# GNN kernel on one core: the table of places for W's products in 16-bit integers

## The reference

```python
edge_index = jnp.stack([src, dst])
h = jnp.maximum(_layernorm(x), 0.0)
# L0: row, col = edge_index
W = jnp.zeros((1024, 1024)).at[row, col].add(edge_weight)
x = x + h @ W.T + L0_gnn_bias
h = jnp.maximum(_layernorm(x), 0.0)
# L1, twice with its own weights (relu between): agg = segment_sum(h[src], dst)
#   h @ W_self + (agg / max(deg, 1)) @ W_neigh + b
x = x + L1_gnn(h, src, dst, ...)
```

## Time and profile before

| | |
|---|---|
| median of 3 runs | 769.54 us (769.11 to 769.72) |
| the profiled execution | 768.53 us |
| its span, first to last instruction | 766.5 us |
| granted TensorE clock in it | 1.0 of full speed, in every slice |
| PE busy | 747.6 us, 98% of the span |
| DVE, POOL, ACT busy | 75%, 62%, 46% |

### The profile page before, as it was taken

The page is one execution under the profiler, slowest core; times in us unless marked ns, Lnnn a source line. Parts: engine busy times, 40 slices in busy tenths (PEclk is TensorE's granted clock), DMA queues, the critical chain, the costliest instruction groups (busy, mean ns, idle before and its releaser), DMA issues.

```text
span 766.5 us, 13521 instructions
## 1 busy us (share of the span) xinstructions
PE 747.6 (98%) x4453; PEld 620.8 (81%) x4454; DVE 572.1 (75%) x819; ACT 353.5 (46%) x593; POOL 473.6 (62%) x593
## 2 busy tenths in 40 slices
PE   3999999999999999999999999999999999999998
PEld 2878888888888888888788888888888888887887
DVE  7999677877465797986779685446598857569885
ACT  7977623433353452366336745542223323245731
POOL 3000366667579999865656373436999875645992
PEclk9999999999999999999999999999999999999999
DMA  3123467665586854567683536776743868785475
GB/s 117 50 74 111 115 217 257 204 227 179 167 289 198 295 157 133 172 218 253 211 271 116 165 120 197 253 247 208 272 142 104 254 199 286 234 288 185 144 235 202
DMA packets 82984, 148.78 MB, mean 194 GB/s; under 512 B 10809, under 2 KB 21108, under 8 KB 82912
## 3 DMA queue, kind: packets, MB, share of 16 engines
q1 hardware_dynamic: 62974, 105.18, 44.0%
q10 hardware_dynamic: 19938, 42.69, 15.8%
HBM read 106.42 MB, written 41.41 MB: 193 GB/s over the span
## 4 chain that ended last, share of the span: by engine, by line
PE 97%; DVE 2%; issue 1%; DMA 0%; DVEq 0%
PE bank L1765 50%; PE bank L1819 21%; PE bank L1690 14%; PE bank L1575 4%; PE bank L1563 1%; PE bank L1596 1%; PE bank L1837 1%; PE bank L1586 1%; PE bank L1681 1%; PE bank L1592 1%; DMA dst_g<-in_dst 0%; DVE L L2004 0%; DVE R L1989 0%; PE bank L1604 0%; DVE low L1883 0%
## 5 line engine op out<-in xcount | busy, mean ns | idle before, releaser
L1765 PE MATMUL bank<-slot,split 128*128 128x512 f32 x1128 | 261.7, 390 | 0.5 <-issue 0.5
L1765 PEld LDWEIGHTS bank<-slot,split 128*128 128x128 f32 x1128 | 210.9, 188 | 44.2 <-issue 0.9
L1085 POOL TENSOR_TENSOR AT<-AT,az 128x50 int32 (+3 forms) x288 | 94.6, 329 | 115.8 <-DMA az<-asum_scratch 72.9
L1765 PE MATMUL bank<-slot,split_third 128*128 128x512 f32 x552 | 129.7, 390 | 0.0
L1765 PEld LDWEIGHTS bank<-slot,split_third 128*128 128x128 f32 x552 | 103.1, 188 | 21.4 <-issue 0.2
L1819 PE MATMUL bank<-slot,Ax 128*128 128x512 f32 (+1 forms) x510 | 119.1, 388 | 0.3
L1819 PEld LDWEIGHTS bank<-slot,Ax 128*128 128x128 f32 x510 | 93.4, 188 | 20.0 <-issue 1.4
L2149 DVE TENSOR_TENSOR slot<-T,slot 128x512 fp32r<-128x512 f32 x64 | 84.3, 1328 | 25.9 <-ACT slot L1348 22.0
L1690 PE MATMUL bank<-slot,split_m 128*128 128x512 f32 x320 | 87.9, 396 | 0.0
L1141 POOL TENSOR_TENSOR T<-T,wst 128x512 f32<-128x512 f32 x48 | 65.1, 1375 | 4.9 <-DMA wst<-in_L_gnn_W_self 4.9
L1690 PEld LDWEIGHTS bank<-slot,split_m 128*128 128x128 f32 x320 | 58.5, 188 | 11.4 <-issue 0.2
(11 more groups left out here) (234 smaller groups left out, 1196.2 us busy)
## 6 DMA issues: line engine op xcount, KB each, us to landing
stage<-hT_scratch SPq DMA_DIRECT2D x90, 256.0 KB, 3.8
wst<-in_L_gnn_W_neigh SPq DMA_DIRECT2D x56, 256.0 KB, 4.6
wst<-in_L_gnn_W_self SPq DMA_DIRECT2D x56, 256.0 KB, 3.6
x1b_scratch<-x ACTq DMA_DIRECT2D x10, 512.0 KB, 5.6
hT_scratch<-hTs ACTq DMA_DIRECT2D x10, 512.0 KB, 3.1
wst<-prod0g_scratch SPq DMA_DIRECT2D x20, 256.0 KB, 3.5
hT_scratch<-h1s ACTq DMA_DIRECT2D x20, 256.0 KB, 3.3
wst<-prod1g_scratch SPq DMA_DIRECT2D x20, 256.0 KB, 3.4
```

What stands on the lines that cost most here:

```text
L1085: pool.tensor_tensor(a, a, az32[:, n % NZ, pairs * pos:pairs * (pos + 1)], ALU.add) \
L1765: last = pe.matmul(dense_bank(v, which)[:, :], split_tile(v, a)[:, NT * k:NT * (k + 1)], slot[t % 2][:, b, HF * (HK * which + k):HF * (HK ...
```

## The change

`tab_o` holds unsigned 16-bit integers in place of 32-bit ones, and DVE writes them into a tile of their own, `tab_go`, rather than into the first 8 columns of `tab_g`. PE's load of a group's eight places then covers 16 bytes in place of 32. The program has the same instructions in the same order on every engine; only the two operands' names and the type differ. The tiles that are placed behind `tab_o` in SBUF move down by 608 or 640 bytes.

```diff
-        tab_o = sb("tab_o", [1, NG * GC], I32, build)
+        tab_o = sb("tab_o", [1, NG * GC], U16, build)
...
         tab_g = sb("tab_g", [NG, COLS], I32, build)
+        tab_go = sb("tab_go", [NG, GC], U16, build)
...
             sp.wait_ge(s_tab, 1)
-            sp.dma_start(tab_o[:, :], tab_g[:, OFFW:OFFW + GC]).then_inc(s_tabo, 16)
+            sp.dma_start(tab_o[:, :], tab_go[:, :]).then_inc(s_tabo, 16)
...
             dve.wait_ge(s_dve, shifted)
-            dve.tensor_scalar(tab_g[:, OFFW:OFFW + GC], shift[:, :], float(TW), None, ALU.mult).then_inc(s_tab, 1)
+            dve.tensor_scalar(tab_go[:, :], shift[:, :], float(TW), None, ALU.mult).then_inc(s_tab, 1)
```

## The result

The changed kernel takes 817.51 us (median of 6 runs, 816.89 to 819.15), the kernel before 769.33 us beside it (767.93 to 770.66). The ratio is 1.0628, with a 95% interval of 1.0613 to 1.0643: some 48 us slower. The profiled execution took 816.89 us with a span of 814.8, 48.3 more than before.

What follows compares the result with a forecast made beforehand. The prediction took PE, paced in the build by its sequencer and loads, as the bound, with DVE a floor just below. Shorter loads, capped by DVE, give 1.65 us: 769.54 - 1.65 = 767.9 us, range 767.4 to 770.2.

Steps and rivals of the forecast that it cites:

- What bounds the kernel: Build, 8 to 79 us: PE's sequencer, not its columns, sets the pace; DVE is a floor 1.68 us below.
- The load: PE's 35 eight-place loads, groups 2 to 36: from 587 to about 340 ns each, 250 less.
- I take bytes as the likelier: PE's load: its steps of some 260 ns go by 16 bytes begun rather than by four values.
- The slower rival: PE's loads: a 16-bit value is fetched by itself or has a second pass; 778.7 to about 824 us; chance 0.18.
- full form: Slower case, PE's loads: each of eight values one step, 2143 ns, 54 us more in 35 loads, about 824 us.
- Each ns is paid 35 times: Slower case: PE is already slower than DVE, so no cap helps; 44 ns more per load is measurable.
- The cap by DVE: Build's end: PE catches up with DVE, so group 36 starts only 1.63 us sooner, not 7.8.
- After that PE has no wait that could swallow the gain: Behind L1681, the build's end: the 1.65 us gained reaches the end of the span.
- The floor and the price by registers: Skill's rules for PE's load, under the unchanged-load rival: about 600 ns floor, or some 200 ns per register; 769.5 us; chance 0.33.

Runs made afterwards that it cites:

- The two kernels at DVE's floor: Kernel before, 32-bit table: four places loaded, each used twice, 767.74 us against 769.00; eight loaded, only four used, each twice, 768.02 against 768.91.

## Why the prediction was wrong, step by step

**What bounds the kernel: right.** PE's sequencer sets the pace of the build, each group waits for its load, and the end of the build passes to the end of the span: 47.96 us of longer loads became 48.3 us of span.

**The load, the step that failed:** "I take bytes as the likelier", and with it "a group's eight places are one step ... about 340 ns". They took 1922. Two readings went into it. The staircase of 304, 587 and 848 ns was read as one step for each four values or 16 bytes begun. It is a step for each whole block of four, and a trip for a value left over; with one, eight and nine values in the rows, none of them with a rest of two or three, the two can't be told apart. And the choice between values and bytes left out that the block might be tied to the word: every table in the trace was of 32-bit words at multiples of 16 bytes, so the rows carried no price for anything else.

**The slower rival: right in its mechanism,** with its full form at 824 us; it was given too little, 0.18, with the trace having nothing against it. Its size was off in one term: the further trip was taken from the step between eight and nine values, 261 ns, and it is 232 (297 to 1919 ns in seven further trips). 35 x (1.92 - 0.59) is 46.6 us, and the loads that something delayed (up to 2384 ns) bring it to 48. "Each ns is paid 35 times" held.

**The cap by DVE: right in place and size,** 1.63 us forecast and 1.61 measured once a load took one trip, with 0.05 us between DVE's end and PE's start. It had no part in the result.

**"After that PE has no wait that could swallow the gain": not decided.** Later builds passed through to the end: in eight kernels, with builds of up to 50 us later, it is 686.3 to 686.8 us from W's turn on. The two kernels at DVE's floor waited 1.6 and 1.7 us later on, and their medians kept 1.26 and 0.89 us of 1.61. But both use four places twice, and the kernels with that edit and a later build lose time there too. No run has the earlier build without the edit.

**The floor and the price by registers.** The Trainium skill's page "DMA: Bandwidth & Descriptors", in "Latency and other measured facts", has a floor of about 600 ns for such a load; with 297 and 334 ns measured, these loads have no such floor. The Trainium skill's page "Runtime: NRT & Kernel Launch", in "Instruction fetch mechanics", has some 200 ns a register, written of the loads that the runtime puts around a kernel. I had counted it for no change, since the number of registers stays. By that rule eight values are 1.6 us (an estimate), and that is near what a load pays that isn't fetched in blocks (1.92 us, some 230 ns each); for aligned 32-bit blocks it doesn't hold (594 ns for eight). Read as the price outside the case that the trace showed, it would have warned.

## What to carry to other kernels

A load of registers is priced by its form, and bytes saved were no time saved here: keep tables that a sequencer reads in 32-bit words, begin each read at a multiple of 16 bytes, and read whole fours (four cost 334 ns, two cost 534). Where the trace shows an operation in one form only, a change of form has no price in it; measure it alone, at the end of the program, before it goes into a loop. And where an experiment leaves work out, look at how the stages that it should not touch have changed: here they took 1.2 to 3.5 us more.

## What was not expected of the hardware

PE's load of two or three 32-bit values takes longer than one of four (534 and 767 against 334 ns), and an aligned load of four hardly more than one of a single value (301).

A register instruction that computes a place costs PE 0.067 to 0.075 us in the build, where the sequencer is the bound; one of those that take words apart, 0.15 on the average.

The granted clock reads 1.00 from 60 to 78 us in the kernel after, the array standing a good part of the time (a windows row, then two rows of PE's timeline):

```profile
core 0: us, PE busy (x) PEld busy (x) DVE busy (x) ACT busy (x) POOL busy (x), PEclk, DMA share, GB/s
...
60.00:78.00 18.00, 13.88 (x189) 10.71 (x190) 10.50 (x16) 6.57 (x17) 0.00 (x0) 1.00 0.12 41
```

```profile
76.53 0.63 PE L1593 MATMUL bank<-none 125*128 125x512 bf16 x1
...
78.86 0.38 PE L1593 MATMUL bank<-none 125*128 125x512 bf16 x1
```

Yet the clearing matmul of 512 columns took 0.63 us each time until the one at 76.53 us, and 0.38 from 78.86 on. In the kernel before it goes from 0.63 to 0.38 earlier, between 34.27 and 37.89 us. If the longer time is that of the lower level, 1.2 GHz, the rows of the clock don't show it. It cost nothing that the time shows, since 47.96 of 48.3 us are the loads' own. Why the profile's two readings differ stays open.
